# Other units loaded in blocks, another order of the opening, one load of the centroids, and a halved last output group

## The reference

```python
xn = x / max(norm(x, axis=1), EPS);  cn = centroids / max(norm(centroids, axis=1), EPS)
sim = einsum('bchw,nc->bnhw', xn, cn)
idx = argmax(sim, axis=1)                                # nearest of N=40 centroids, per pixel
onehot = one_hot(idx, N)
sum_x = einsum('bhwn,bchw->bnc', onehot, x);  count = sum(onehot, axis=(1, 2))
centroids_local = sum_x / max(count, 1)[..., None]       # mean of the pixels of each cluster
gathered = centroids_local[b, idx]                       # per pixel, back to (B, C, H, W)
delta = gathered - x
alpha = exp(-mean(delta * delta, axis=1))
y = x + alpha * delta
out = relu(einsum('oc,bchw->bohw', W, y) + b)
```

## Time and profile before

| | us |
|---|---|
| median of 3 runs | 414.05 (414.0 to 414.16) |
| the profiled execution | 413.94 |
| its span, in the profile | 412.2 |
| PE busy | 406.1 (99%) |
| DVE / ACT / POOL busy | 333.7 / 257.9 / 262.9 |

### The profile page before, as it was taken

One profiled execution on the slowest core, in us unless ns is written; L12 is line 12 of the kernel. 1 busy time (PEld: TensorE's weight loads), 2 busy tenths in 40 slices (PEclk: granted clock), 3 DMA queues, 4 the chain that ended last, 5 costly groups with the idle time before them and its releaser, 6 DMA issues.

```text
span 412.2 us, 5764 instructions
## 1 busy us (share of the span) xinstructions
PE 406.1 (99%) x2085; PEld 289.7 (70%) x2085; DVE 333.7 (81%) x407; ACT 257.9 (63%) x355; POOL 262.9 (64%) x117
## 2 busy tenths in 40 slices
PE   9999999999999999999999999999999999999996
PEld 6756475775777677775867758776777758777885
DVE  2439998788889879899798889898798996898730
ACT  6566772767665674665865576655846657576542
POOL 2003872994699676993889946995769937433420
PEclk9999999999999999999999999999999999999999
DMA  7992493997599396966879485994966240222223
GB/s 258 375 252 51 92 252 87 275 252 158 192 248 259 113 252 164 277 158 181 260 194 251 169 172 185 258 241 125 259 156 212 104 141 2 102 102 103 102 81 124
DMA packets 77823, 74.59 MB, mean 181 GB/s; under 512 B 13716, under 2 KB 52628, under 8 KB 77796
## 3 DMA queue, kind: packets, MB, share of 16 engines
q1 hardware_dynamic: 77796, 74.23, 64.6%
HBM read 46.30 MB, written 25.17 MB: 173 GB/s over the span
## 4 chain that ended last, share of the span: by engine, by line
PE 94%; DVE 3%; POOL 1%; ACT 1%; issue 0%; ACTq 0%; DVEq 0%; POOLq 0%
PE main L970 21%; PE main L971 20%; PE main L972 20%; PE fa L865 11%; PE sump L910 8%; PE gat L948 5%; PE fa L874 1%; PE al L954 1%; PE main L1032 1%; PE al L1010 1%; PE main L985 1%; DVE xr L468 1%; POOL o L370 1%; PE gat L985 1%; DVE z L462 1%; POOL o L373 1%
## 5 line engine op out<-in xcount | busy, mean ns | idle before, releaser
L970 PE MATMUL main<-yh,wh 128*128 128x512 f32 x376 | 153.2, 408 | 0.0
L971 PE MATMUL main<-yl,wh 128*128 128x512 f32 x376 | 146.8, 390 | 0.0
L972 PE MATMUL main<-yh,wl 128*128 128x512 f32 x376 | 146.6, 390 | 0.0
L348 POOL TENSOR_TENSOR z<-z,x 128x1024 f32<-128x1024 f32 x41 | 98.5, 2422 | 69.0 <-DVE z L495 69.0
L355 POOL TENSOR_TENSOR yl<-z,yh 128x1024 fp32r<-128x1024 f32 x43 | 103.6, 2426 | 8.1 <-ACT yh L657 8.1
L665 ACT ACTIVATE o<-main,bcol 128x512 f32<-128x512 f32 x96 | 65.4, 683 | 59.9 <-PE main L972 59.7
L970 PEld LDWEIGHTS main<-yh,wh 128*128 128x128 f32 x376 | 70.6, 188 | 21.6 <-issue 4.6
L972 PEld LDWEIGHTS main<-yh,wl 128*128 128x128 f32 x376 | 70.6, 188 | 15.2
L971 PEld LDWEIGHTS main<-yl,wh 128*128 128x128 f32 x376 | 70.7, 188 | 14.0
L362 POOL TENSOR_TENSOR xr<-xt 128x2048 f32<-128x2048 f32 x11 | 51.5, 4677 | 18.2 <-DVE xt L399 18.2
L462 DVE TENSOR_TENSOR z<-gat,x 128x1024 f32<-128x1024 f32 x46 | 55.9, 1214 | 5.3 <-PE gat L948 5.2
(11 more groups left out here) (130 smaller groups left out, 393.4 us busy)
## 6 DMA issues: line engine op xcount, KB each, us to landing
out<-o SPq DMA_DIRECT2D x23, 1024.0 KB, 7.4
x<-x SPq DMA_DIRECT2D x21, 1024.0 KB, 5.7
xs<-x SPq DMA_DIRECT2D x76, 256.0 KB, 5.5
x<-x SPq DMA_DIRECT2D x12, 256.0 KB, 4.6
o<-w SPq DMA_DIRECT2D x1, 1024.0 KB, 9.1
out<-o SPq DMA_DIRECT2D x4, 256.0 KB, 2.0
sq<-centroids SPq DMA_DIRECT2D x2, 80.0 KB
oht<-oh SPq DMA_TRANSPOSE x7, 3.7
```

What stands on the lines that cost most here:

```text
L348: pool.tensor_tensor(z, z, X[g // PARTS % 2][:, pair(h), span(g)], ALU.add).then_inc(y_pool, 1)
L970: t_.matmul(main[:, o % 2, :], WH[:, k, rows], YH[g % 2][:, k, :], start=(k == 0), stop=False)
L971: t_.matmul(main[:, o % 2, :], WH[:, k, rows], YL[g % 2][:, k, :], start=False, stop=False)
L972: last = t_.matmul(main[:, o % 2, :], WL[:, k, rows], YH[g % 2][:, k, :], start=False, stop=(k == KC - 1))
```

## The change

- `EARLY = 2`: only units 0 and 1 are transposed by TensorE in the opening; unit 2 is loaded in blocks (`load_xs(2)`, ahead of the loads of units 3 to 5) and transposed by DVE. TensorE turns units 3 and 5, and unit 4 comes in blocks. `load_xs` now waits for the transpose of whichever unit used its buffer last (`shares_blocks`).
- `turn` has four steps; that of unit 3's last tiles uses the banks `al` and `sump`.
- Centroids are loaded once, and both squarings read the same rows. One `keep_busy` instead of two stands ahead of the similarities.
- Orders: the similarities of unit 2 stand ahead of the second half of unit 0's transposes; unit 0's two `scale` stand between the two `delta` of unit 1; `y_half(0, 0)` goes to POOL, the second `add_chunks` of unit 1 to DVE; `transpose_half(6, 0)` moves from ahead of `delta(3, 0)` to behind it; the sum of squares of unit 1 moves in between the first convolution matmuls.
- The last output group of unit 23 is computed in two halves of 256 columns, in two banks; ACT and DVE take one each, and each is stored by itself.

```diff
+EARLY = 2
+TURNED = (PARTS, PARTS + 2)
+TURNS = ((PARTS, (0, 1)), (PARTS + 2, (0, 1)), (PARTS, (2, 3)), (PARTS + 2, (2, 3)))
...
-    return g == 0 or (g == 1 or g >= TAIL) and h == 1
+    return (g < LAG or g >= TAIL) and h == 1
...
+def shares_blocks(g):
+    return max((i for i in range(EARLY, g) if i not in TURNED and (g - i) % 2 == 0), default=None)
...
             def load_xs(g):
-                if blocks_loaded(g) > 1:
-                    wait(sp, tr_done, by_vector(g - 2))
+                if shares_blocks(g) is not None:
+                    sp.wait_ge(tr_done, by_vector(shares_blocks(g)))
...
-            sp.dma_start(craw[column_tiles[0], :], cent).then_inc(c_in[0], 16)
+            sp.dma_start(craw[0:N, :], cent).then_inc(c_in, 16)
...
+            load_xs(2)
             load_x(3)
             load_x(4)
             load_x(5)
-            load_xs(3)
+            load_xs(4)
             load_xs(6)
             transpose_onehot(1)
             load_xs(7)
...
             first_best(0)
+            transpose_half(2, 0)
+            transpose_half(2, 1)
             low_weights(0)
             low_weights(1)
             low_clusters(0)
...
             delta(0, 1)
-            transpose_half(3, 0)
+            transpose_half(4, 0)
             best_sims(1)
             first_best(1)
             delta(1, 0)
+            scale(0, 0)
+            transpose_half(4, 1)
             delta(1, 1)
-            transpose_half(3, 1)
-            scale(0, 0)
-            y_half(0, 0)
             scale(0, 1)
             y_half(0, 1)
+            add_chunks(1, 1)
             low_clusters(1)
+            delta(2, 0)
             scale(1, 0)
+            counts(1)
             scale(1, 1)
-            counts(1)
-            delta(2, 0)
             y_half(1, 1)
             delta(2, 1)
...
-            transpose_half(6, 0)
             for g in range(PARTS, UNITS):
...
                 delta(g, 0)
                 if g == PARTS:
+                    transpose_half(g + 3, 0)
                     transpose_half(g + 3, 1)
...
+            dve.wait_ge(main_done, KC * UNITS + 1)
+            v_.tensor_scalar(OUT[g % 2][:, KC - 1, UNIT // 2:UNIT], second_half, bcol[:, KC - 1:KC], 0.0, ALU.add,
+                             ALU.max).then_inc(last_done, 1)
...
-            keep_busy(2)
+            keep_busy(1)
...
             similarities(0)
             transpose_x(0, 0)
             similarities(1)
+            similarities(2)
             transpose_x(0, 1)
-            similarities(2)
+            transpose_sims(0)
             transpose_x(1, 0)
-            transpose_sims(0)
             transpose_x(1, 1)
-            transpose_x(2, 0)
-            transpose_x(2, 1)
             transpose_weights(0)
             transpose_weights(1)
+            transpose_weights(2)
             pe.wait_ge(const_done, 7)
             sum_clusters(0, 0)
             sum_clusters(0, 1)
+            transpose_onehot()
             sum_clusters(0, 2)
-            transpose_onehot()
-            transpose_weights(2)
+            transpose_weights(3)
+            pe.wait_ge(x_in[1][0], 16)
+            turn(0)
             add_halves(0)
-            transpose_weights(3)
-            pe.wait_ge(x_in[1][1], 16)
-            turn(0)
...
             gather(2, 0)
-            sum_squares_direct(1)
-            pe.wait_ge(z_done, 4)
             pe.wait_ge(hi_done, 1)
             high_passes(range(0, 2))
+            sum_squares_direct(1)
             pe.wait_ge(hi_done, 2)
             high_passes(range(2, KC))
...
+            for half in range(2):
+                convolve(UNITS - 1, KC - 1, slice(half * UNIT // 2, (half + 1) * UNIT // 2))
```

More of the change, by code:

```diff
@@ L78, in sum_order @@
 def sum_order(b):
-    return (0, 1, 2) if b == 0 else (1, 2, 0) if b == 1 else (2, 0, 1)
+    return (0, 1, 2) if b == 0 else (0, 2, 1) if b == 1 else (2, 0, 1)
 def by_vector(g):
-    return sum(i not in TURNED for i in range(PARTS, g + 1))
+    return sum(i not in TURNED for i in range(EARLY, g + 1))
+def shares_blocks(g):
+    return max((i for i in range(EARLY, g) if i not in TURNED and (g - i) % 2 == 0), default=None)
 def blocks_loaded(g):
-    return sum(i not in TURNED and (g - i) % 2 == 0 for i in range(PARTS, g + 1))
+    return sum(i not in TURNED and (g - i) % 2 == 0 for i in range(EARLY, g + 1))
 def folded(g):
@@ L174, in build @@
         w_in, b_in = sem("w_in"), sem("b_in")
-        c_in = [sem(f"c_in{j}") for j in range(2)]
+        c_in = sem("c_in")
         out_done = [sem(f"out_done{j}") for j in range(2)]
@@ L312, in _ @@
             g = UNITS - 1
-            for o in range(KC):
+            for o in range(KC - 1):
                 sp.wait_ge(relu_done, KC * g + o + 1)
@@ L316, in _ @@
                              ).then_inc(out_done[g % 2], 16)
+            at, rows = span(g).start, slice((KC - 1) * P, C)
+            sp.wait_ge(relu_done, KC * UNITS)
+            sp.dma_start(out[BATCH - 1, rows, at:at + UNIT // 2], OUT[g % 2][:, KC - 1, 0:UNIT // 2]
+                         ).then_inc(out_done[g % 2], 16)
+            sp.wait_ge(last_done, 1)
+            sp.dma_start(out[BATCH - 1, rows, at + UNIT // 2:at + UNIT], OUT[g % 2][:, KC - 1, UNIT // 2:UNIT]
+                         ).then_inc(out_done[g % 2], 16)
             sp.wait_ge(out_done[1 - g % 2], 16 * (UNITS // 2))
-            sp.wait_ge(out_done[g % 2], 16 * (UNITS // 2 - 1 + KC))
+            sp.wait_ge(out_done[g % 2], 16 * (UNITS // 2 + KC))
         @block.gpsimd
@@ L364, in first_rest, with add_chunks @@
                                    ).then_inc(rest1_done, 1)
[L366 to L376, removed]
+            def add_chunks(g, h):
+                sq = squares(g, h)
+                pool.wait_ge(sq_done, 2 * g + h + 1)
+                pool.tensor_tensor(sq[:, 0, :], sq[:, 0, :], sq[:, 1, :], ALU.add).then_inc(two_done, 1)
+            add_chunks(0, 0)
+            add_chunks(0, 1)
+            pool.wait_ge(two_done, 2)
+            first_two, last_two = squares(0, 0)[:, 0, :], squares(0, 1)[:, 0, :]
+            pool.tensor_tensor(first_two, first_two, last_two, ALU.add).then_inc(four_done, 1)
+            y_half(0, 0)
+            add_chunks(1, 0)
             for g in range(UNITS):
-                y_half(g, 0)
-                y_half(g, 1)
+                if g > 0:
+                    y_half(g, 0)
+                    y_half(g, 1)
                 low_half(g, 0)
@@ L626, in keep_turned @@
                 g, tiles = TURNS[step]
-                act.wait_ge(xp_done, PARTS * 2 + step + 1)
-                a_.activation(XT[:, g % PARTS, tiles[0]:tiles[-1] + 1, :], turn_bank(tiles), ACT.Copy
-                              ).then_inc(xe_act, 1)
+                act.wait_ge(xp_done, 2 * EARLY + step + 1)
+                if step == 2:
+                    for t, bank in zip(tiles, turn_banks(step)):
+                        last = a_.activation(XT[:, g % PARTS, t, :], bank, ACT.Copy)
+                    last.then_inc(xe_act, 1)
+                else:
+                    a_.activation(XT[:, g % PARTS, tiles[0]:tiles[-1] + 1, :], gat[:, :, :], ACT.Copy
+                                  ).then_inc(xe_act, 1)
             def square(g, h):
@@ L837, in _ @@
             relu(g - 1, 3)
-            for o in range(KC):
+            for o in range(KC - 1):
                 relu(g, o)
+            relu(g, KC - 1, slice(0, UNIT // 2))
         @block.tensor
@@ L960, in sum_squares_direct, with convolve @@
                           ).then_inc(one_done, 1)
-            def convolve(g, o, ks=range(KC)):
-                if ks[0] == 0:
-                    wait(pe, relu_done, KC * g + o - 1)
+            def convolve(g, o, cols=slice(0, UNIT)):
+                wait(pe, relu_done, KC * g + o - 1)
                 rows = slice(o * P, (o + 1) * P)
-                for k in ks:
+                tile = main[:, o % 2, cols] if cols.start == 0 else second_half
+                for k in range(KC):
                     if o == 0 and k % 2 == 0:
@@ L969, in convolve @@
                         wait_low(pe, g, k // 2)
[L970 to L975, removed]
+                    t_.matmul(tile, WH[:, k, rows], YH[g % 2][:, k, cols], start=(k == 0), stop=False)
+                    t_.matmul(tile, WH[:, k, rows], YL[g % 2][:, k, cols], start=False, stop=False)
+                    last = t_.matmul(tile, WL[:, k, rows], YH[g % 2][:, k, cols], start=False, stop=(k == KC - 1))
+                last.then_inc(main_done, 1)
             def transpose_x(u, half):
@@ L1002, in turn @@
                     for k in range(KC):
[L1003 removed]
+                        last = t_.transpose(turn_banks(step)[i][:, k * P:(k + 1) * P], X[1][:, k, at:at + P],
                                             ident[:, :])
```

91 lines of the change are left out of this document (44 added, 47 removed).

## The result

The changed kernel takes 418.32 us (median of 5, 417.4 to 419.33), the kernel before 414.0 beside it: ratio 1.0105, interval 1.0087 to 1.0122. The execution profiled took 417.4 us, its span is 415.6.

What follows compares the result with a forecast made beforehand. TensorE's own work was taken to bound the kernel from 66 to 409 us, so only opening (-1.45) and tail (-0.3) count: -1.75 from 413.94, with the median 0.1 above, gives 412.3 us; range 410.4 to 414.0.

Steps and rivals of the forecast that it cites:

- The moved chunk addition costs DVE 0.6 + 0.6.: Before unit 1's sum of squares: additions moved from POOL to DVE were taken at 0.6 us each.
- one microsecond: At `y_half(0, 0)` on POOL: blocking between POOL and DVE would add 1 us, said to be already inside the sum.
- the 44.75: Forecast end in us of `y_half(0, 0)` on POOL, taken at 3.0 us, two microseconds before DVE had it.
- C: Rival: one-hot DMA lands late behind `load_xs(6)`, delaying relu and TensorE; at 54.6 it costs 1.65, 415.7 us; chance 0.08.
- The one-hot DMA: Batch 1, behind four xs DMAs: lands at 51.3, bounds 49.2 and 54.6; TensorE waits 1.7 us for the first relu.
- 2.3 us "until any packet lands": In the one-hot landing sum: startup time subtracted from that DMA's 3.8 us to get its own packets' time.
- the gains of 1.75: Opening 1.45 us sooner at the gather of unit 3's second half, plus 0.3 at the tail.
- Unit 2's blocks: Opening loads queued behind W: landed at 21.1 (21.1 to 22.1); TensorE waits 0.6 us ahead of the third sum.
- rival B: Blocks of unit 2 or unit 4 land 1 to 1.5 us later, moving all behind: about 413.5 us; chance 0.20.
- The tail: Halved last output group: DVE 0.28 less, store 0.15 less, 24 matmuls of 256 columns 0.1 more; sum -0.3 us.
- rival D: Halved last group bounded by weight loads, one matmul every 0.19 us: +1.8 on the forecast, 414.1 us; chance 0.05.
- Idle in the loop: After the opening: TensorE was forecast not to idle after 65 us, so gains there last to the end.

Runs made afterwards that it cites:

- e1: Changed kernel with POOL held back from unit 0's two low halves until unit 1's squares are added: 413.41 us, ratio 1.0001 to the kernel before.
- e10: Changed kernel with the second half of unit 1's squares in PSUM, so each DVE addition reads one SBUF operand; POOL not held back: 413.73 us, ratio 1.0015.
- e8: Kernel before with only the second and third addition of unit 1's squares moved from POOL to DVE, behind `y_half(0, 1)`: 420.4 us, ratio 1.0158.
- e3: Changed kernel with 18 idle products on TensorE in place of its wait for unit 1's squares: 415.99 us, ratio 1.0059.
- e7: Changed kernel with the one-hot DMA of batch 1 issued ahead of `load_xs(6)`, nothing else: 419.13 us, ratio 1.0135.
- e5: e1 with the one-hot DMA of batch 1 issued ahead of `load_xs(6)`: 412.75 us, ratio 0.9994.
- e2: Changed kernel with all three additions of unit 1's squares on POOL again: 414.09 us, ratio 1.0011.
- e9: e5 with DVE's `counts(1)` ahead of `delta(2, 0)` and ACT's count ahead of `exp(1)`: 412.55 us, ratio 0.9984.
- e11: e10 with the one-hot DMA ahead of `load_xs(6)`, DVE's `counts(1)` ahead of `delta(2, 0)`, ACT's count ahead of `exp(1)`; POOL not held back: 412.19 us, ratio 0.9971.
- e12: e11 with the bias load behind `load_xs(2)` instead of ahead of it: 411.82 us, ratio 0.9958.

## Why the prediction was wrong

**The step that failed** is this one: "The moved chunk addition costs DVE 0.6 + 0.6." It costs 2.86 + 2.71. The prediction had the two things it needed for that: the 2.29 us of an addition of the same form beside POOL, and the rule of the Trainium skill (SBUF — State Buffer, "SBUF: two separate sides") that of two such operations the second waits for the whole of the first. But it applied them to `y_half(0, 0)` on POOL, and gave the whole effect one microsecond. It did not lay POOL's own timeline beside the additions: with unit 0's first half 2 us sooner, POOL's low halves begin near 46.9, when the additions do. The trace agrees with the rule: both additions end 0.55 us behind a low half. e1 (POOL away, additions 0.68) and e10 (an operand in PSUM, 0.68) show the cause, and in e8 the part alone costs 6.9 us. The microsecond was also misplaced in its sum: 3.0 was taken for `y_half(0, 0)` and 3.40 is the bound, so the 44.75 had room for 0.4 us, not for 1.

**What the wait is worth** was missing altogether: behind 4.3 us of idleness the clock halves. e3 sets 1.9 to 2.3 us on it, the rows 2.2 (5.0 for 2.8). Together some 6.5 us at the sum of squares. Not all of it stands in the time: the change's gains up to that place give some back, and without the wait others appear. So e1, which removes both parts, is only 4.9 us below the changed kernel, 4.3 by the ratios; TensorE waits there 0.5 us for POOL's late low half and 1.1 for the relu. None of the rivals named this mechanism; C had the right sign for another reason.

**Up to 45.9 us** the working was right in kind and nearly in size: similarities, sums, turned copies, the early half on POOL (2.38 us, where 3.0 was taken; it ends at 44.54 for 44.75). The means were some 0.5 later than taken (31.46 for 31.0), and the gather and the sum of squares of unit 0 were 0.7 and 0.6 late.

**The one-hot DMA** landed at 51.7 (forecast 51.3), 6.5 us after its issue: right in size. The 2.3 us "until any packet lands" in that sum stand in no row: in the trace of the kernel before the DMA engines were at work 1.3 us after the issue (from 46.9). That the sum met the landing within 0.4 us is partly luck. In the changed kernel it is hidden by the late sum of squares (e7). In e1, without that, TensorE waits 1.1 us for the first relu and the second gather is at 65.33, forecast 64.7. But the DMA is only half of it: e5's trace shows that behind it DVE's order (counts behind `scale(1, 0)`) held the same relu. Rival C's sum is off by 0.1: the gains of 1.75 are gone at 51.3 + 1.75 = 53.05, not at 52.95.

**Unit 2's blocks** (rival B): they were forecast for 21.1 and DVE starts on them at 21.19. Over the profiles this start moves, and the gather of unit 2 with it, nearly microsecond for microsecond once TensorE waits:

| | DVE starts on the blocks | TensorE waits at the third sum | first gather of unit 2 |
|---|---|---|---|
| e1 | 20.93 | 0 | 45.60 |
| after | 21.19 | 0.44 | 45.69 |
| e2 | 21.73 | 1.01 | 46.22 |
| e3 | 22.18 | 1.26 | 46.68 |
| e10 | 22.42 | 2.0 | 46.92 |
| e9 | 22.66 | 1.99 | 48.55 |

e5, e7 and e11 fit in between (21.23 and 45.72; 21.62 and 46.12; 21.38 and 45.87). e9 is 1.87 behind e3 where its blocks are 0.48 later; the other 1.4 is the clock's part (the third sum takes 3.32 us instead of 1.94). That the forecast of 412.3 isn't reached by e1 (413.4 in the median, 412.74 in the profiled execution) may go with this: the profiled execution had the earliest blocks of all. That most others had later ones isn't shown, since one execution of each kernel was traced. What sets the landing from run to run stays open; e12 tried one reason and didn't show it.

**The tail** was forecast at -0.3, is -0.4 in the traces, with 0.12 us between matmuls: the 2.4 us estimated by the rule of the Trainium skill (TensorE: Matmul & The Clock Gate, "The mechanism") did not come, nor did rival D. DVE's half takes 0.48, for 0.41. In medians it isn't resolved.

**Idle in the loop**: none came (PE busy 336.93 of 337 us from 72 to 409); what was lost or won by 70 us stayed to the end, as forecast.

## What to carry to other kernels

Before a VectorE operation with two SBUF operands is moved, lay GpSimd's timeline beside its new place: it may wait until a whole GpSimd operation ends, four times its own length here. Putting one operand in PSUM removed that wait without touching the order (e10; with two more waits removed e11, at 0.9971 of the kernel before, a gain of 1.2 us by the ratio). And price a wait on TensorE by its length and by the clock behind it: behind 4.3 us of waiting, work of 2.8 us took 5.0.

## What was not expected of the hardware

A wait of 1.99 us in the opening (e9) was followed by a fall of the granted clock to 0.50, where one of 2.0 us at the same place (e10) and those of 1.26 and 1.29 us (e3, e2) left it at 1.00: two executions with the same wait differ by 1.4 us. A single part of the change, two additions, made the kernel before 6.9 us slower (e8). And the landing of the same four DMAs, issued from 8 us on, moved by up to 1.7 us between executions of kernels alike up to there (DVE starts on them at 20.93 in e1, at 22.66 in e9).
